# Relative values: four query shifts a group with the table's high and low halves side by side; one exponential for two PSUM banks

## What is computed

```
rel_pos = jnp.arange(L)[None, :] - jnp.arange(L)[:, None] + (MAX_LEN - 1)
rel_k = relative_k[rel_pos]
rel_v = relative_v[rel_pos]
scores = jnp.einsum('bhld,bhrd->bhlr', Q, K) * scale
scores = scores + jnp.einsum('bhld,lrd->bhlr', Q, rel_k)
attn = jax.nn.softmax(scores, axis=-1)
out = jnp.einsum('bhlr,bhrd->bhld', attn, V)
out = out + jnp.einsum('bhlr,lrd->bhld', attn, rel_v)
```

## Time and profile before

| | |
|---|---|
| median of 3 runs | 3464.99 us (3463.78 to 3466.43) |
| profiled execution, first to last instruction | 3463.7 us |
| busy: PE, DVE, ACT, POOL | 3194.2, 2813.3, 2634.6, 2262.5 us |
| attention, by the relative key products | 169.8 to 2849.6 us |

### The profile page before, as it was taken

How to read it: one execution, slowest core, us unless ns; L and a number is a source line. 1 busy time by engine, 2 the same in 40 slices (tenths; PEclk the granted TensorE clock), 3 DMA queues, 4 the chain that set the end, 5 groups by cost and what they waited for, 6 DMA issues and landing times. The chain is left out here.

```text
span 3463.7 us, 165894 instructions
## 1 busy us (share of the span) xinstructions
PE 3194.2 (92%) x64918; PEld 2524.8 (73%) x64918; DVE 2813.3 (81%) x7853; ACT 2634.6 (76%) x5852; POOL 2262.5 (65%) x2526
## 2 busy tenths in 40 slices
PE   7589999999999999999999999999999996999990
PEld 4357777777777777777777777777777785579980
DVE  6479999999999999999999999999999986534443
ACT  3288888888888888888888888888888893234440
POOL 0167777777777777777777777777777774700006
PEclk9779999999999999999999999999999997589995
DMA  7776666666666666666666666666666664712224
GB/s 212 228 230 216 221 220 221 221 221 224 218 221 224 221 223 224 222 218 224 221 223 224 223 217 221 224 224 221 224 218 222 222 217 161 239 51 69 62 62 145
DMA packets 356374, 701.28 MB, mean 202 GB/s; under 512 B 59545, under 2 KB 168706, under 8 KB 355346
## 3 DMA queue, kind: packets, MB, share of 16 engines
q1 hardware_dynamic: 349458, 673.92, 60.3%
q0 software_dynamic: 6144, 16.79, 1.5%
HBM read 343.02 MB, written 347.46 MB: 199 GB/s over the span
## 5 line engine op out<-in xcount | busy, mean ns | idle before, releaser
L850 POOL TENSOR_TENSOR pt_near<-pt_full,pt_near 128x512 f16<-128x512 f32 (+3 forms) x1984 | 1857.7, 965 | 583.8 <-DVE pt_near L1170 583.8
L1077 ACT ACTIVATE pt_full<-pb,exp_bias 128x512 f32<-128x512 f32 x2048 | 1313.5, 688 | 305.7 <-PE pb L960 183.9
L1011 PEld LDWEIGHTS pb<-pt_near,table_high 128*128 128x128 f16 x18432 | 794.6, 97 | 145.1 <-issue 106.4
L1011 PE MATMUL pb<-pt_near,table_high 128*128 128x64 f16 (+6 forms) x18432 | 884.8, 187 | 15.7 <-DVE rel_out L1203 14.6
L1150 DVE TENSOR_REDUCE part_max<-pb 128x1 f32<-128x512 f32 (+3 forms) x1376 | 771.2, 574 | 131.0 <-PE pb L918 130.0
L1011 PE MATMUL pb<-pt_near,table_low 128*128 128x64 f16 (+6 forms) x9216 | 851.4, 187 | 0.0
L1011 PEld LDWEIGHTS pb<-pt_near,table_low 128*128 128x128 f16 x9216 | 772.7, 97 | 0.0
L1146 DVE CUSTOM_DVE_ANT_0 near_sum<-pb,skewed 128x512 bf16<-128x512 f32 (+3 forms) x1216 | 675.6, 571 | 109.4 <-PE pb L918 85.0
L952 PE MATMUL pb<-ident,skewed 128*128 128x128 f32 x3840 | 621.6, 285 | 20.5 <-ACT q_max L1101 19.2
L1170 DVE CAST pt_near<-pt_full 128x512 f16<-128x512 f32 (+3 forms) x1280 | 532.3, 466 | 0.3 <-PE pb L984 0.3
L984 PE MATMUL pb<-v_head,pt_near 128*128 128x33 f16 x13440 | 507.2, 178 | 9.1 <-POOL pt_near L850 5.5
(11 more groups left out here) (182 smaller groups left out, 4063.3 us busy)
## 6 DMA issues: line engine op xcount, KB each, us to landing
skewed<-rel_scratch SPq DMA_DIRECT2D x256, 576.0 KB, 5.3
rel_scratch<-rel SPq DMA_DIRECT2D x416, 319.5 KB, 3.4
rel_scratch<-rel SPq DMA_DIRECT2D x320, 320.0 KB, 2.8
skewed<-rel_scratch SPq DMA_DIRECT2D x64, 512.0 KB, 4.6
skewed<-rel_scratch SPq DMA_DIRECT2D x64, 448.0 KB, 4.3
k_stack<-planes_scratch SPq DMA_DIRECT2D x192, 96.0 KB, 4.7
planes_scratch<-planes SPq DMA_DIRECT2D x64, 256.0 KB, 2.3
rel_scratch<-rel SPq DMA_DIRECT2D x64, 256.0 KB, 2.7
```

The source lines that it names most:

```text
L850: ins = nc.gpsimd.tensor_tensor(pt_piece(c, 1, a, z, near), pt_full[e][:, (a - 4 * g) * P:(z - 4 * g) * P], pt_piece(c, 0, a, z, near), AL ...
L1011: ins = nc.tensor.matmul(acc[:, c0:c1, :], keep[table][:, w:w + P], pt_near[half][:, part, c0:c1, d - M_LO, a * SHIFTS:(a + 1) * SHIFTS], ...
L1077: nc.scalar.activation(pt_full[e][:, :], x_ps[e % 2][:, :], ACT.Exp, bias=exp_bias[:, 0:1]).then_inc(s_exp, 1)
```

## The change

Relative values: `SHIFTS` is 4, and the 128 columns of weights are now 4 shifts x 2 parts (table high, table low) x 16. High and low probabilities stand side by side in the moving operand: 2 parts x 8 tiles x 4 queries, again at most 64 columns. One matmul does what three did (and a fourth product, low with low, besides). A half has 32 groups of 9 matmuls, 288. In the bank, the sums of the high and the low probabilities stand apart, so ACT first copies the low one to `rel_low` and DVE adds the other to it into `rel_out` (`join_values`), four times a half; the mask is POOL's, in place, twice a half (`mask_values`). Values are turned one step later (`LAG_SEL`).

Exponentials: one instruction for both banks of a pair, 1024 elements, with the constant as a number of the instruction and not as a column of a tile.

```diff
-SHIFTS = P // DK
+PARTS = 2
+PART_D = PARTS * DK
+SHIFTS = P // PART_D
 SHIFT_GROUPS = P // SHIFTS
+BANK_GROUPS = CH // (PARTS * HALF_C * SHIFTS)
+FLUSHES = SHIFT_GROUPS // BANK_GROUPS
+FLUSH_STEPS = HALF_C // FLUSHES
...
-LAG_SEL = LAG_RV + HALF_C
+LAG_SEL = LAG_RV + HALF_C + 1
...
+            def mask_values(it, h, part):
+                pool.wait_ge(s_rle, FLUSHES * h + FLUSHES // 2 * (part + 1))
...
+                nc.gpsimd.tensor_tensor(vals, vals, mask.to_broadcast([P, HALF_C, half_a, SHIFTS]), ALU.mult).then_inc(s_rlm, 1)
...
-                    if 4 * u + e >= 2 and (near[e] or e % 2):
-                        pe.wait_ge(s_exp, it * (4 * STEP) + 4 * u + e - 1)
+                    if 2 * u + pair >= 1 and e % 2 == 0:
+                        pe.wait_ge(s_exp, 2 * u + pair)
...
-                    for n, (table, part) in enumerate((("table_high", 0), ("table_high", 1), ("table_low", 0))):
...
+                    ins = nc.tensor.matmul(
+                        acc[:, :, c0:c1, :], keep["table_pair"][:, w:w + P],
+                        pt_near[half][:, :, c0:c1, d - M_LO, a * SHIFTS:(a + 1) * SHIFTS],
...
-                first = 2 if rel_on and j else 0
+                first = 2 if rel_on and j % FLUSH_STEPS else 0
...
-            def exponentials(it, u, e):
-                act.wait_ge(s_x[e % 2], it * (2 * STEP) + 2 * u + e // 2 + 1)
-                if u >= 1:
-                    wait_low(act, it, u - 1, e)
-                nc.scalar.activation(pt_full[e][:, :], x_ps[e % 2][:, :], ACT.Exp, bias=exp_bias[:, 0:1]).then_inc(s_exp, 1)
+            def exponentials(it, u, pair):
+                for i in range(2):
+                    act.wait_ge(s_x[i], 2 * u + pair + 1)
+                    if u >= 1:
+                        wait_low(act, it, u - 1, 2 * pair + i)
+                nc.scalar.activation(pt_pair[pair][:, :, :], x_pair[:, :, :], ACT.Exp, bias=PROB_SCALE_LN).then_inc(s_exp, 1)
...
+            def take_low(it, h, f):
+                act.wait_ge(s_rl, FLUSHES * h + f + 1)
+                src = r_ps[:, :].rearrange("p (a r x) -> p r a x", r=PARTS, x=HALF_C * SHIFTS)[:, 1, :, :]
+                nc.scalar.copy(rel_low[:, :, :], src).then_inc(s_rlc, 1)
...
-            def mask_values(it, h, part):
-                dve.wait_ge(s_rl, it * (2 * HALF_STEP) + 2 * h + part + 1)
...
-                nc.vector.tensor_tensor(dst, src, mask.to_broadcast([P, half_a, HALF_C, SHIFTS]), ALU.mult).then_inc(s_rle, 1)
+            def join_values(it, h, f):
+                dve.wait_ge(s_rlc, FLUSHES * h + f + 1)
...
+                nc.vector.tensor_tensor(dst, src, low, ALU.add).then_inc(s_rle, 1)
```

More of the change, by code:

```diff
@@ L332, in step @@
                     sp.nop(nofuse=True)
[L333 to L337, removed]
+                    for a, n, col in ((LEFT0, LEFT_N, 0), (MAIN0, MAIN_N, LEFT_N)):
+                        src = bass.AP(hbm["table"].tensor, (a - LEFT0) * PART_D, [[PART_D, P], [1, n * PART_D]])
+                        sp.dma_start(keep["table_pair"][:, col * PART_D:(col + n) * PART_D], src).then_inc(s_tbr, 16)
                     sp.wait_ge(s_rkp, 2)
@@ L573, in attend @@
         ident_half = sb("ident_half", [P, P], FP16)
-        exp_bias = sb("exp_bias", [P, 1])
-        pt_full = [sb(f"pt_full{i}", [P, CH]) for i in range(E)]
+        pt_pair = [sb(f"pt_full{i}", [P, 2, CH]) for i in range(E // 2)]
+        pt_full = [pt_pair[e // 2][:, e % 2, :] for e in range(E)]
         pt_near = [sb(f"pt_near{i}", [P, 2, HALF_C, REL_BLOCKS, P], FP16) for i in range(2)]
@@ L871, in step @@
                         low_part(it, u, e)
+                for part in range(2):
+                    h, j = half_at(k, LAG_RV + HALF_C // 2 * (part + 1))
+                    if j == 0 and h >= 0 and exists(it, h * HALF_C):
+                        mask_values(it, h, part)
                 h, j = half_at(k, LAG_O)
@@ L1000, in rel_values @@
                         wait_low(pe, it, u, E - 1)
[L1001 to L1007, removed]
-                    c0, c1 = half_range(half, d)
-                    w = table_window(d, a) * DK
-                    for n, (table, part) in enumerate((("table_high", 0), ("table_high", 1), ("table_low", 0))):
[L1011 to L1015, removed]
+                a = 4 * j + quarter
+                g = a % BANK_GROUPS
+                ds = (0, 1, -1, -2, 2, -3, -4, -5, -6)
+                acc = r_ps[:, :].rearrange("p (a r c b) -> p a r c b", r=PARTS, c=HALF_C, b=SHIFTS)[:, g, :, :, :]
+                for d in ds:
+                    c0, c1 = half_range(half, d)
+                    w = table_window(d, a) * PART_D
+                    ins = nc.tensor.matmul(
+                        acc[:, :, c0:c1, :], keep["table_pair"][:, w:w + P],
+                        pt_near[half][:, :, c0:c1, d - M_LO, a * SHIFTS:(a + 1) * SHIFTS],
+                        start=(g == 0 and d == ds[0]), stop=(g == BANK_GROUPS - 1 and d == ds[-1]))
+                if j % FLUSH_STEPS == FLUSH_STEPS - 1 and quarter == 3:
                     ins.then_inc(s_rl, 1)
@@ L1108, in step @@
                     exponentials(it, k - LAG_X, 0)
-                    exponentials(it, k - LAG_X, 1)
+                for f in range(FLUSHES):
+                    h, j = half_at(k, LAG_RV + FLUSH_STEPS * (f + 1))
+                    if j == 0 and h >= 0 and exists(it, h * HALF_C):
+                        take_low(it, h, f)
                 if exists(it, k - LAG_A):
@@ L1115, in step @@
                 if turning:
-                    exponentials(it, k - LAG_X, 2)
-                    exponentials(it, k - LAG_X, 3)
+                    exponentials(it, k - LAG_X, 1)
                 if exists(it, k - LAG_A):
@@ L1241, in step @@
                     search_bank(it, a, 2)
+                for f in range(FLUSHES):
+                    h, j = half_at(k, LAG_RV + FLUSH_STEPS * (f + 1))
+                    if j == 0 and h >= 0 and exists(it, h * HALF_C):
+                        join_values(it, h, f)
                 if exists(it, k - LAG_PV):
```

71 lines of the change are left out of this document (36 added, 35 removed).

## The result

The changed kernel takes 3633.36 us (median of 4 runs, 3628.82 to 3634.01) where the kernel before takes 3465.71 beside it: 1.0481 times as long, 95% interval 1.0467 to 1.0495. That is 168 us slower, outside the range; 3445 was forecast.

A forecast was written before the change was run, and what follows sets the result against it. The prediction took PE alone to set the pace before the change. Pair loop -5, PE's waits for masked values -38 and POOL's mask +21 made -22 us from 3465, 3443, stated as 3445; range 3300 to 3525.

The forecast's parts named there:

- The mask, priced at +21: POOL's 128 mask products, 1.3 us each: 42 us if all of one per head shows, half taken, 21 us slower.
- one of the four per head falls into the steps in which POOL also makes value parts and is late anyway: On POOL, the only mask per head charged: 1.3 us times 32 heads, 42 us, bounds 0 and 84.
- The loop of the pairs: Two-step attention loop through POOL, ACT, PE and DVE: 5.00 us a step against 5.01 measured, so 5 us gained in all.
- 10.07: Predicted us for the two-step loop with 36 relative matmuls on PE and no join: 2.33 + 1.06 + 4.16 + 1.96 + 0.56.
- 9.94: Predicted us for the two-step loop with 18 relative matmuls on PE and a join, 0.35 of it not overlapped.
- Rival 2: First pair's exponential waits for POOL's second low part; loop longer than today's step, 46 us slower, 3510; chance 0.27.
- PE alone set the pace: Attention's quiet stretch: PE paces steps at 5.01 us; 18 fewer matmuls save 0.49 a step, 250 us if PE alone counted.
- rival 1: In attention, the loop has slack and DVE is the bound: 215 us go, 3250, up to 3360; chance 0.23.
- PE's wait for masked values: PE waits for DVE to mask values before refilling their bank: 28.6 us in 380 steps, 38 in all, should go.
- The constant: Exponential on ACT without a bias operand: 1.00 us for 1024 elements, lowering ACT's load; no term in the sum.
- Rival 3: Shorter runs slow PE's relative matmuls: at twice 0.027 us each, some +220 to +250 us, 3690 to 3715; chance 0.05.

## Why the prediction was wrong

The runs make a ladder; each step is the difference of two ratios times 3465 us, good to some 8 us:

| kernel | ratio | step, us |
|---|---|---|
| before | 1 | |
| constant in the instruction | 0.9913 | -30 |
| one product of three left out | 0.9773 | -49 |
| new relative values, no mask | 0.9823 | +17 |
| mask on POOL (relative values alone) | 1.0182 | +124 |
| pairs: the changed kernel | 1.0481 | +104 |

1. **The mask, priced at +21, cost 124.** This is the largest wrong term, and the step that failed is "one of the four per head falls into the steps in which POOL also makes value parts and is late anyway". I charged POOL's lateness in one step of four masks and took POOL's idle time for free. But DVE's cast and low part are held while the product runs: 42 us of casts and 34 of low parts, over all shapes, in the run of the relative values alone against that without the mask, and POOL's next low parts wait for those casts. Of the 123 masks that the changed kernel's trace lists apart, 30 run straight on into value parts, which are the ones that I charged; behind the other 93 POOL sits idle until DVE has made a cast. PE hardly waits for the masked values: 2.1 us, once. The Trainium skill has the rule, on its page "SBUF — State Buffer" (Who interferes with whom): VectorE's casts, where they run in a mode that uses two ports, and its operations with two inputs in SBUF beside a GpSimd instruction that reads SBUF, share a pair of ports with GpSimd, and whoever comes second waits for the whole instruction. The trace agrees: 1.13 us in the timeline above for a low part that takes 0.28 alone. I didn't weigh that rule.
2. **The loop of the pairs, "10.07" and "9.94", was too short.** Its place was right: with the mask on POOL, two sets of tiles take away all that the pairs cost, and the 228 us that ACT waits for POOL all stand before first pairs. But I closed it for the first pair and POOL only. The second pair waits for DVE's low part three, 97 us in 2000, behind two searches and the join; that branch isn't in the sum. Added up again in the changed kernel, from POOL's start at 1591.68 to 1603.40, the terms are 2.87 + 1.07 + 4.42 + 2.80 + 0.56 = 11.72 for 10.07 (ACT's exponential starts at 1594.55, PE's transposes at 1595.62, DVE's search at 1600.04, its cast at 1602.84). The largest miss is DVE's stretch, 2.80 for 1.96, which holds the long low part of the timeline above. The next loop, 1597.83 to 1608.66, is 10.83 for 9.94, with 4.33 for 3.68 on PE: there PE waits for the cast of the query, which stands on ACT behind an exponential that waited for low part three:

```profile
1603.04 1.02 ACT L1098 ACTIVATE pt_full<-px 128x1024 f32<-128x1024 f32 x1 [0.80 <-DVE pt_far L1207]
1603.95 0.26 ACT L1122 CAST q_max<-pb 128x128 f16<-128x128 f32 x1
```

```profile
1604.27 0.66 PE L975 MATMUL px<-ident,skewed 128*128 128x128 f32 x4 [0.45 <-ACT q_max L1122]
```

In the two runs that have pairs and no join, the wait for low part three is 20 and 17 us, and pairs cost 44 and 53; in the changed kernel without its mask it is 59, and they cost 108. No run takes away the second pair's wait alone, so its share is argued and not shown. The changed kernel without the mask takes 1.0135, 47 us more. Rival 2 named the place and a price of 46 us; that the price fits is luck, since it was made of an exponential of 1.17 us, which took 1.025, and of a POOL late by 0.5. With the mask the place is the same and the loss 168.
3. **"PE alone set the pace" was wrong.** 0.49 us a step off the relative matmuls is worth 49 us by itself, not 250. PE was busy 97% of the stretch, and still each of its steps waited for a round trip through three others. So rival 1 (DVE the bound, 3250) was wrong as well: DVE's own time shows to a third.
4. **PE's wait for masked values** is gone as forecast: 28.6 us in the stretch before, 3.6 in the whole span after. But its 38 us can't be added to the rest; it was idle time of an engine that waits elsewhere now. With copy and join in its place the balance is +17.
5. **The constant** I priced at nothing beyond ACT's load; alone it gave 30 us. The estimate of 1.04 us from the Trainium skill's page "ScalarE: Activation LUTs" (What ACT_TABLE_LOAD costs) agrees with 1025 ns.
6. **Rival 3** is out. Relative matmuls of the changed kernel, a batch of 18:

```profile
1500.02 0.64 PE L1031 MATMUL pr<-pt_near,table_pair 128*128 128x64 f16 x18
```

The last one's own time is some 0.19 us of the 0.64; 17 spacings in the other 0.45 are 0.026 each, as before, where 26 took the 0.70 from 1507.07 to 1507.77. So the rule of "PSUM — Partial Sum Buffer" (Specifications) in the Trainium skill on non-contiguous patterns doesn't show here: the sums that go to two runs, at the ends of the window, stream like those that went to one.

That the mask's product costs 38, 73 and 124 us is partly a matter of cover, of other work that hides it: the first rise comes from fewer matmuls alone. The second comes with the join, the copy and the later turning; which of them, no run tells. My sum took the clock to stay at 1.00. In the stretch it is 1.00 without a mask, 0.98 with it and 0.97 with the pairs too, so some of these two steps of the ladder comes through the clock, which fell behind PE's waits; how much, no run tells apart.

## What to carry to other kernels

Idle time of GpSimd wasn't free here where VectorE was casting or subtracting in SBUF at that moment: before moving work there, lay the two timelines over each other. In a chain of engines that wait for each other within a step, busy shares didn't price an edit; a spare instruction at the spot came nearer, and its price changed with each other edit. Add up every branch that a joined wait brings in, not only the one that is late today.

## Not expected of the hardware

VectorE's 128x128 low part under a GpSimd product: 1076 ns for 279. An add of 32 partitions and 64 elements costs VectorE 267 ns, so four small ones cost 2.5 times one of 128x256 (422 ns). ScalarE with a column as scale, on 128 elements four apart, takes 553 ns, about as long as a cast of 128x384 (529).
